# A convolution, scan and attention block on one core: the delta bias as a 49th row of the delta product, and the products of delta and x on GpSimd

## The chip, the cores and the metric

The kernel runs on one core of one Trainium2 chip. The metric is device time in microseconds (us): the median of several executions, without the host. The core has five engines that run side by side and wait for one another through semaphores: TensorE (PE in the profile), VectorE (DVE), ScalarE (ACT), GpSimd (POOL) and SyncE (SP, which issues the transfers here). SBUF is the memory on the chip in which the operands lie. PSUM is the smaller one into which TensorE writes; it has eight banks of 128 x 512 floats.

## The reference, cut to what matters

The block is a state-space layer, then attention, then a mixture of experts. The change lies in the state-space layer. There `x` is convolved and put in four orders (`K = 4`; by rows, by columns, and both backwards). For each order a small matrix gives the step sizes `delta`, through a product of inner size `R = 24`, a bias and a softplus:

```python
x_dbl = jnp.einsum('bkdl,kcd->bkcl', xs, x_proj_w)
dts, Bs, Cs = jnp.split(x_dbl, [R, R + N], axis=2)
dts = jnp.einsum('bkrl,kdr->bkdl', dts, dt_projs_w)
dts = jax.nn.softplus(dts + dt_projs_b[None, :, :, None])
...
dA = jnp.exp(d_t[..., None] * As)
h = h * dA + (d_t * u_t)[..., None] * B_t[:, :, None, :]
```

The scan needs two arrays of it: `delta` and `delta * x`.

## The kernel before

Two images stand side by side on the 128 partitions, so there are two pairs of images (`p` = 0 and 1, `NP = 2`). A pair has 12 **halves** (`HALVES`): one of the four orders and one third of the 192 channels each. A half is 128 partitions by 1024 positions. The 24 halves of both pairs are numbered `m`. They are made in one stretch of the program, called the **delta stage** here; it stands between the input projection with its convolution and the scan.

One half goes through these steps. The lines are those of the profile.

- TensorE multiplies 48 rows of weights (24 for each of the two images) with 48 rows of `rows` into one of two pairs of PSUM banks, `DT_PS[m % 2]` (`delta_product`, L1167). This is two matmuls of 512 columns, and the profile counts four passes, since they are float32.
- ScalarE reads the banks twice, with the bias as an operand: the absolute value goes to `u_mk` (L767), and a biased copy goes to `d_mk` (L768). The copy raises `dt_evacuated`; TensorE waits for it before it fills the same banks for half `m + 2`.
- ScalarE takes exp(-u) (L773). One is added to it, by ScalarE in every third half (`one_more`, L782) and by VectorE in the others (L1618). VectorE keeps what rounding lost (`lost_part`, L1621), ScalarE takes the logarithm (`log_w`, L787).
- VectorE adds max(d, 0) and the logarithm (L1628), subtracts the lost part (L1631), and multiplies with `x` (L1635). SyncE stores both results to HBM (L422, L424), in four buffers (`MADE`).

Softplus is thus max(v, 0) + log(1 + exp(-|v|)).

The order on every engine is written out by hand, in loops over `p` and over a step `s`, and nothing is reordered. Between the halves the same loops carry other work. TensorE makes the rows for the next products and for B and C (`x_proj`, L1139, 12 passes), seven taps of one convolution (`conv`, L1123, 14 passes), and takes away parts that ScalarE has split off (`take_hi`, `take_mid`, L1147). ScalarE splits B and C into three bfloat16 parts (L747, L748, L752, L756), copies `rows` (L737), and once goes through a SiLU block with two table loads (L843 to L846). GpSimd turns `x` by columns (L575). Ahead of the stage VectorE makes the other taps of the convolution (L1572, L1586), and the transfers of the constants, the last of them the four of `xproj_w` (L394), must all have landed before L1650 on VectorE. The tables `HI_AT`, `DT_ROWS_AT`, `BC_ROWS_AT` and `CONV_AT` say after which half each of these stands.

Behind the delta stage follows the scan, 384 units on all engines. VectorE scans (L1705), GpSimd multiplies inputs (L587) and readouts (L604), TensorE spreads B and C (L1213) and adds up (L1229).

Of the kernel before, what the change touches and what calls it, by code (L numbers as in the profile page):

```python
# [5 lines left out]
ALU = mybir.AluOpType  # L6
# [12 lines left out]
H2 = P // 2  # L19
J = DI // H2  # L20
# [3 lines left out]
PART = 3  # L24
DR = 2 * R
SR = 2 * N
BR = PART * SR
# [131 lines left out]
def hybrid_block_kernel(nc, a, out):  # L159
    with ExitStack() as ctx:  # L160
# [21 lines left out]
        a_neg = always.take(OJ, 2, N)  # L182
        dt_bias = always.take(OJ, 2, 1)
        d_sum = always.take(OJ, 1)
# [125 lines left out]
        def attend_bank(i):  # L310
# [13 lines left out]
        ab_ok, u_ok, w_ok, pd_ok = sem("abs_ready"), sem("u_ready"), sem("w_ready"), sem("delta_uncorrected")  # L324
        dtev_ok, lost_ok, ln_ok = (sem(n) for n in ("dt_evacuated", "lost_part", "ln_ready"))
        xd_ok, xa_ok = sem("dt_rows_filled"), sem("bc_rows_filled")
# [36 lines left out]
        CONSTS = [  # L363
            (ident, "ident"), (ones, "ones"), (a_neg, "a_logs"), (dt_bias, "dt_bias"), (d_two, "ds"),
            (conv_b, "conv_b"), (norm_g, "norm_g"), (norm_b, "norm_b"),
# [14 lines left out]
        def _(sp):  # L380
# [181 lines left out]
        def _(pool):  # L562
# [9 lines left out]
            def by_columns(p, j):  # L572
# [109 lines left out]
        def _(act):  # L682
# [74 lines left out]

            def dt_out(p, i):
                k, j, q, dr = half_of(p, i)
                m = p * HALVES + i  # L760
                bias = dt_bias[:, q % OJ, dr, :]
                act.wait_ge(dt_ok, m + 1)
                if m >= MADE:
                    act.wait_ge(dm_st[m % MADE], m // MADE * 32)
                elif m == BLANK_FROM:
# [9 lines left out]
            def one_more(p, i):  # L775
                m = p * HALVES + i
                act.wait_ge(u_ok, m + 1)
                if m:
                    act.wait_ge(pd_ok, m - 1)
                else:  # L780
                    act.wait_ge(xc_ok, J)
                nc.scalar.activation(w_mk[:, m % 2], u_mk[:, m % MADE], ACT.Identity, bias=ones[:, 0:1]).then_inc(w_ok, 1)  # L782
# [280 lines left out]
        def _(pe):  # L1063
# [95 lines left out]
            def delta_product(p, i):  # L1159
                k, j, q, dr = half_of(p, i)  # L1160
                m = p * HALVES + i
                lo = H2 * dr
                pe.wait_ge(rows_ok, p * 2 + k % 2 + 1)
                if m >= 2:
                    pe.wait_ge(dtev_ok, m - 1)
                for h in range(2):
                    mm = pe.matmul(DT_PS[m % 2][:, h * 512:(h + 1) * 512], dt_w[lo:lo + DR, q % OJ, dr],  # L1167
                                   rows[lo:lo + DR, k % 2, h * 512:(h + 1) * 512], start=True, stop=True)
                mm.then_inc(dt_ok, 1)
# [92 lines left out]
            pe.wait_ge(rows_ok, 2 * NP)  # L1262
            pe.wait_ge(dtev_ok, NP * HALVES)
            tile_steps(0, True, False)
# [252 lines left out]
        def _(dve):  # L1517
# [90 lines left out]
            def lost_part(p, i):  # L1608

                m = p * HALVES + i  # L1610
                u, w = u_mk[:, m % MADE], w_mk[:, m % 2]
                if i % J:
                    dve.wait_ge(u_ok, m + 1)
                    if m >= 2:
                        dve.wait_ge(pd_ok, m - 1)
                    else:
                        dve.wait_ge(xc_ok, J)
                    chain.link(nc.vector.tensor_scalar(w, u, 1.0, None, ALU.add))  # L1618
                else:
                    dve.wait_ge(w_ok, m // J + 1)  # L1620
                nc.vector.scalar_tensor_tensor(out=u, in0=w, scalar=-1.0, in1=u, op0=ALU.add, op1=ALU.subtract).then_inc(lost_ok, 1)  # L1621

            def finish(p, i):
                k, j, q, dr = half_of(p, i)
                m = p * HALVES + i
                d, u = d_mk[:, m % MADE], u_mk[:, m % MADE]
                dve.wait_ge(ln_ok, m + 1)
                nc.vector.scalar_tensor_tensor(out=d, in0=d, scalar=0.0, in1=w_mk[:, m % 2],  # L1628
                                               op0=ALU.max, op1=ALU.add).then_inc(pd_ok, 1)
# [21 lines left out]
            for tap in range(PE_TAPS):  # L1651
                nc.vector.tensor_scalar(conv_diag[:, tap], ident, conv_w[:, J - 1, tap:tap + 1], None, ALU.mult)
            nc.vector.tensor_scalar(minus, ident, -1.0, None, ALU.mult)
            nc.vector.tensor_tensor(d_sum.rearrange("p q one -> p (q one)"), d_two[:, 0], d_two[:, 1], ALU.add).then_inc(setup, 1)
            group_var(2)
# [508 lines left out]
```

## Time and profile before

| | |
|---|---|
| time, median of 3 runs | 2245.13 us (2244.14 to 2249.29) |
| span of the profiled execution, first to last instruction | 2244.7 us |
| delta stage in it, from the first L767 to the first product of the scan on VectorE | 95.37 to 253.46 us, 158.1 us |
| VectorE busy in the delta stage | 136.08 us |
| ScalarE busy in the delta stage | 131.63 us |
| TensorE busy in the delta stage | 124.09 us, at a mean granted clock of 0.74 |
| GpSimd busy in the delta stage | 5.68 us |

The profiled execution has no other time than its span; the span lies 0.4 us under the median of the runs. A granted clock of 1.00 is 2.4 GHz for TensorE, and 0.50 is 1.2 GHz. Times in the rows count from the start of the span.

### The profile page before, as it was taken

What the parts mean: (1) busy time and instruction counts of PE and PEld (TensorE: products, weight loads), DVE (VectorE), ACT (ScalarE), POOL (GpSimd) and SP (SyncE); (2) the same over time, 40 slices, a digit from 0 to 9 for tenths busy, and PEclk for the clock granted to TensorE, in tenths of its full rate; (3) what the DMA queues carried; (4) which work ended last, traced back from release to release, by engine and by line L of the source; (5) the groups of instructions that cost most, each with busy time, mean ns of one, the idle gap of its engine ahead of it and who ended that gap; (6) DMA issues with size and microseconds to landing.
All of it is one profiled execution on the core that took longest, in us unless ns stands there. A gap on an engine that the chain in (4) does not pass through costs nothing.

```text
span 2244.7 us, 20167 instructions
## 1 busy us (share of the span) xinstructions
PE 1984.1 (88%) x5826; PEld 919.6 (41%) x5830; DVE 1575.2 (70%) x1505; ACT 1144.9 (51%) x1258; POOL 1297.0 (58%) x464
## 2 busy tenths in 40 slices
PE   7988588888888888888888888989995999999997
PEld 3332133333333333333333333456653555555554
DVE  6978999999999999999999999774553000000000
ACT  4788666666776676776767666211213112122111
POOL 0110499999999999999999999401233011111110
PEclk9987599999999999999999999999997999999999
DMA  6448622233222233222232220611226233333300
GB/s 193 151 175 280 212 75 75 70 98 79 84 66 65 75 100 91 65 75 75 61 105 67 77 73 19 229 42 57 85 85 223 85 119 124 123 119 126 126 24 7
DMA packets 82402, 229.13 MB, mean 102 GB/s; under 512 B 14031, under 2 KB 40257, under 8 KB 80816
## 3 DMA queue, kind: packets, MB, share of 16 engines
q1 hardware_dynamic: 76208, 211.54, 29.6%
q0 software_dynamic: 6144, 16.98, 2.1%
q8 instruction: 24, 0.39, 0.1%
q14 instruction: 26, 0.21, 0.0%
HBM read 166.39 MB, written 64.03 MB: 103 GB/s over the span
## 4 chain that ended last, share of the span: by engine, by line
PE 46%; DVE 23%; issue 17%; POOL 8%; ACT 3%; DMA 1%; DVEq 0%; SPq 0%; ACTq 0%; POOLq 0%
DVE arena L1705 15%; PE ps L1489 11%; PE ps L1502 11%; PE ps L1229 6%; POOL arena L604 4%; POOL arena L587 4%; PE ps L1439 3%; PE ps L1213 2%; PE ps L1110 2%; DVE ps L1688 1%; PE ps L1226 1%; PE ps L1139 1%; PE ps L1390 1%; PE ps L1428 1%; DVE arena L1572 1%
## 5 line engine op out<-in xcount | busy, mean ns | idle before, releaser
L604 POOL TENSOR_TENSOR arena<-arena 128x2048 f32<-128x2048 f32 x192 | 868.3, 4533 | 16.6 <-DVE arena L1705 15.7
L1229 PE MATMUL ps<-arena 128*128 128x512 f32 x1536 | 727.7, 596 | 27.7 <-POOL arena L604 27.6
L1705 DVE TENSOR_TENSOR_SCAN arena<-arena,ps 128x1024 f32<-128x1024 f32 x264 | 587.5, 2266 | 0.0
L880 ACT ACTIVATE arena<-ps 128x1024 f32<-128x1024 f32 x384 | 390.7, 1017 | 248.0 <-PE ps L1213 246.1
L1213 PE MATMUL ps<-arena 96*128 (+1 forms) x1296 | 366.7, 384 | 129.3 <-DVE arena L1705 112.7
L1229 PEld LDWEIGHTS ps<-arena 128*128 128x128 f32 x1536 | 288.4, 190 | 287.7 <-issue 194.0
L587 POOL TENSOR_TENSOR arena<-arena 128x1024 f32<-128x1024 f32 x120 | 283.1, 2359 | 103.5 <-DMA arena<-b_rows 103.5
L2066 DVE TENSOR_TENSOR arena<-ps,arena 128x384 f32<-128x384 f32 x32 | 17.8, 557 | 450.4 <-PE ps L1502 450.4
L1688 DVE TENSOR_TENSOR ps<-ps,arena 128x1024 f32<-128x1024 f32 x264 | 309.1, 1216 | 12.6 <-PE ps L1213 12.6
L873 ACT ACTIVATE arena<-arena 128x1024 f32<-128x1024 f32 x264 | 300.8, 1139 | 8.9 <-DVE arena L1705 8.3
L1213 PEld LDWEIGHTS ps<-arena 96*128 96x128 bf16 x1296 | 112.9, 98 | 461.3 <-DVE arena L1705 215.7
L668 POOL DMA_INDIRECT out<-arena x32 | 31.7, 992 | 437.4 <-DVE arena L2071 437.4
L1705 DVE TENSOR_TENSOR_SCAN arena<-ps,arena 128x1024 f32<-128x1024 f32 x120 | 271.5, 2262 | 4.6 <-ACT ps L873 4.2
L1489 PE MATMUL ps<-arena 128*128 128x512 f32 x576 | 250.2, 595 | 0.0
L1502 PE MATMUL ps<-arena 128*128 128x384 f32 x768 | 250.2, 486 | 0.0
L1502 PEld LDWEIGHTS ps<-arena 128*128 128x128 f32 x768 | 145.4, 190 | 101.5 <-issue 3.8
L873 ACT ACTIVATE ps<-arena 128x1024 f32<-128x1024 f32 x120 | 134.1, 1118 | 88.4 <-DVE arena L1705 88.4
L1489 PEld LDWEIGHTS ps<-arena 128*128 128x128 f32 x576 | 110.1, 191 | 136.8 <-issue 134.4
L1041 ACT ACTIVATE arena<-ps,arena 128x512 f32<-128x512 f32 x96 | 66.0, 688 | 176.0 <-PE ps L1489 175.9
L1048 ACT ACTIVATE arena<-arena 128x384 f32<-128x384 f32 x32 | 16.7, 523 | 232.3 <-DVE arena L2066 232.3
L637 POOL TENSOR_TENSOR arena<-arena 128x384 f32<-128x384 f32 x32 | 27.0, 878 | 185.2 <-DVE arena L1863 185.2
L575 POOL COPY arena<-arena 128x1024 f32<-128x1024 f32 x6 | 13.0, 2192 | 134.2 <-ACT arena L729 134.2
(225 smaller groups left out, 1611.9 us busy)
## 6 DMA issues: line engine op xcount, KB each, us to landing
arena<-b_rows SPq DMA_DIRECT2D x240, 256.0 KB, 4.2
arena<-in_w SPq DMA_DIRECT2D x16, 2304.0 KB, 13.3
delta<-arena SPq DMA_DIRECT2D x24, 512.0 KB, 2.9
delta_x<-arena SPq DMA_DIRECT2D x24, 512.0 KB, 3.1
arena<-delta SPq DMA_DIRECT2D x24, 512.0 KB, 3.6
arena<-delta_x SPq DMA_DIRECT2D x24, 512.0 KB, 4.6
slot_in<-arena SPq DMA_DIRECT2D x8, 772.0 KB, 8.1
arena<-slot_in SPq DMA_DIRECT2D x8, 772.0 KB, 18.0
```

What stands on the lines that cost most here:

```text
L587: nc.gpsimd.tensor_tensor(xin[:, x % XRING], xin[:, x % XRING], dux[:, dr], ALU.mult).then_inc(in_ok, 1)
L604: nc.gpsimd.tensor_tensor(hst[:, h:h + 2], hst[:, h:h + 2], c_sb[:, c:c + 2], ALU.mult).then_inc(p2_ok, 2)
L873: nc.scalar.activation(dst, dlt[:, dr], ACT.Exp, scale=a_neg[:, q % OJ, dr, n:n + 1]).then_inc(dec_ok, 1)
L880: nc.scalar.activation(c_sb[:, u % RING], C_PS, ACT.Copy).then_inc(c_free, 1)
L1041: nc.scalar.activation(h_sb[:, m], ps[:, 3 + m % 3, :], ACT.Gelu_apprx_tanh, bias=b1_col[:, e, m:m + 1]).then_inc(hg_ok, 1)
L1213: mm = pe.matmul(dst[:, h * 512:(h + 1) * 512], sel_lhs[0:BR, n], bc[0:BR, q % OJ // J, dr, m, h * 512:(h + 1) * 512], start=True, stop=True)
L1229: mm = pe.matmul(Y_PS[:, h * 512:(h + 1) * 512], ident, hst[:, u % HRING, h * 512:(h + 1) * 512], start=False, stop=(u == UN - 1))
L1439: mm = pe.matmul(ps[:, attend_bank(i), 0:CA], xnT[:, b % 2, t, i * P:(i + 1) * P], w_eff[:, t], start=(t == 0), stop=(t == CT - 1))
L1489: mm = pe.matmul(ps[:, 3 + m % 3, :], w1[s][:, t, m * P:(m + 1) * P], xeT[:, s, t], start=(t == 0), stop=(t == CT - 1))
L1502: mm = pe.matmul(ps[:, 6 + i % 2, 0:C], h_sb[:, m, i * P:(i + 1) * P], w2[s][:, m], start=(m == 0), stop=(m == MT - 1))
L1688: nc.vector.tensor_tensor(x, x, dux[:, dr], ALU.mult).then_inc(p1_ok, 1)
L1705: nc.vector.tensor_tensor_scan(h, f, x, 0.0, ALU.mult, ALU.add).then_inc(sc_ok, 1)
```

## The change

The biased copy is dropped. Instead the bias becomes a 49th row of the weights (`DRB = 49`), against a 49th row of `rows` that is made to be one, so that the product has the bias in it. The two rows of weights are loaded by two strided transfers of single floats. The sum with max(v, 0) now reads the product in PSUM itself (`whole_delta`), so the banks are free when VectorE has read them (`pd_ok`), no longer when ScalarE has copied them. ScalarE adds the one in every half, and its order in a step is absolute value of half s, logarithm of half s-1, exp and one of half s. The product with `x` leaves VectorE: GpSimd makes it, between its copies by columns.

```diff
+            for lo in (DR, H2 + DR):
+                sp.dma_start(dt_w[lo:lo + 1], a["dt_bias"].rearrange("p q r one -> one q r p"),
+                             allow_slow_non_contiguous=True).then_inc(lb_ok, 16)
...
+            def delta_x(p, i):
+                k, j, q, dr = half_of(p, i)
+                m = p * HALVES + i
+                pool.wait_ge(d_ok, m + 1)
+                u = u_mk[:, m % MADE]
+                nc.gpsimd.tensor_tensor(u, d_mk[:, m % MADE], xy[:, q, :], ALU.mult).then_inc(du_ok, 1)
+
+            for j in range(J):
+                by_columns(0, j)
             for p in range(NP):
-                for j in range(J):
-                    by_columns(p, j)
+                for i in range(HALVES):
+                    delta_x(p, i)
+                    if p == 0 and i == HALVES - 2:
+                        for j in range(J):
+                            by_columns(1, j)
...
-                nc.scalar.activation(rows[0:H2 + DR, o], fill_slot("xd", p, o)[0:H2 + DR], ACT.Copy).then_inc(rows_ok, 1)
+                nc.scalar.activation(rows[0:H2 + DRB, o], fill_slot("xd", p, o)[0:H2 + DRB], ACT.Identity,
+                                     bias=one_row[0:H2 + DRB]).then_inc(rows_ok, 1)
...
-                nc.scalar.activation(u_mk[:, m % MADE], DT_PS[m % 2], ACT.Abs, bias=bias).then_inc(ab_ok, 1)
-                nc.scalar.activation(d_mk[:, m % MADE], DT_PS[m % 2], ACT.Identity, bias=bias).then_inc(dtev_ok, 1)
+                nc.scalar.activation(u_mk[:, m % MADE], DT_PS[m % 2], ACT.Abs).then_inc(ab_ok, 1)
...
                     if s < HALVES:
-                        dt_out(p, s)
-                        exp_abs(p, s)
-                        if s % J == 0:
-                            one_more(p, s)
+                        absolute(p, s)
                     if s >= 1:
                         log_w(p, s - 1)
+                    if s < HALVES:
+                        exp_abs(p, s)
+                        one_more(p, s)
...
                 if m >= 2:
-                    pe.wait_ge(dtev_ok, m - 1)
+                    pe.wait_ge(pd_ok, m - 1)
...
+            def whole_delta(p, i):
+
+                m = p * HALVES + i
+                dve.wait_ge(ln_ok, m + 1)
+                nc.vector.scalar_tensor_tensor(out=d_mk[:, m % MADE], in0=DT_PS[m % 2], scalar=0.0, in1=w_mk[:, m % 2],
+                                               op0=ALU.max, op1=ALU.add).then_inc(pd_ok, 1)
...
                 dve.wait_ge(pd_ok, m + 1)
                 nc.vector.tensor_tensor(d, d, u, ALU.subtract).then_inc(d_ok, 1)
-                if k == 1:
-                    dve.wait_ge(xT_ok, (p + 1) * J)
-                dve.wait_ge(d_ok, m + 1)
-                nc.vector.tensor_tensor(u, d, xy[:, q, :], ALU.mult).then_inc(du_ok, 1)
...
             for p in range(NP):
                 for s in range(HALVES + 1):
+                    if s >= 1:
+                        whole_delta(p, s - 1)
                     if s < HALVES:
                         lost_part(p, s)
```

On ScalarE, late in the second pair, where no other work stands between the halves, a step reads like this before. `delta_stored` is the buffer's store, `dt_filled` the product, `lost_part` VectorE's L1621.

```order
L767 ACTIVATE arena<-ps,arena 128x1024 [waits delta_stored1,dt_filled]
L768 ACTIVATE arena<-ps,arena 128x1024
L773 ACTIVATE arena<-arena 128x1024 [waits abs_ready]
L782 ACTIVATE arena<-arena 128x1024 [waits delta_uncorrected,u_ready]
L787 ACTIVATE arena<-arena 128x1024 [waits lost_part]
```

The same place reads like this after the change. L784 is the absolute value, L801 the logarithm of the half before, L789 the exp and L796 the one.

```order
L784 ACTIVATE arena<-ps 128x1024 [waits delta_stored1,dt_filled]
L801 ACTIVATE arena<-arena 128x1024 [waits lost_part]
L789 ACTIVATE arena<-arena 128x1024 [waits abs_ready]
L796 ACTIVATE arena<-arena 128x1024 [waits delta_uncorrected,u_ready]
L784 ACTIVATE arena<-ps 128x1024 [waits delta_stored2,dt_filled]
```

The copy is gone, and the logarithm of a half has moved behind the absolute value of the next half and ahead of its exp. Before, it stood behind both.

On VectorE, at the same place, one half took these rows before.

```order
L1618 TENSOR_SCALAR arena<-arena 128x1024 [waits delta_uncorrected,u_ready]
L1621 SCALAR_TENSOR_TENSOR arena<-arena 128x1024 [waits dve_chain]
L1628 SCALAR_TENSOR_TENSOR arena<-arena 128x1024 [waits ln_ready]
L1631 TENSOR_TENSOR arena<-arena 128x1024 [waits delta_uncorrected]
L1635 TENSOR_TENSOR arena<-arena 128x1024 [waits delta_ready]
```

After the change VectorE has these rows there: `whole_delta`, the lost part, the subtraction, and `whole_delta` of the next half.

```order
L1635 SCALAR_TENSOR_TENSOR arena<-ps,arena 128x1024 [waits ln_ready]
L1629 SCALAR_TENSOR_TENSOR arena<-arena 128x1024 [waits w_ready]
L1643 TENSOR_TENSOR arena<-arena 128x1024 [waits delta_uncorrected]
L1635 SCALAR_TENSOR_TENSOR arena<-ps,arena 128x1024 [waits ln_ready]
L1629 SCALAR_TENSOR_TENSOR arena<-arena 128x1024 [waits w_ready]
```

Five instructions became three, and the sum with the logarithm now reads PSUM and stands ahead of the next half's lost part.

On TensorE the order is the same; what a product waits for is not. Behind the first rows for B and C, where half 2's product stands with the first `take_hi` behind it, the rows were these before.

```order
L1167 MATMUL ps<-arena 128x512 [waits dt_evacuated,rows_copied]
...
L1147 MATMUL ps<-arena 128x512 [waits b_rows_then_hi]
...
L1167 MATMUL ps<-arena 128x512 [waits dt_evacuated,rows_copied]
...
L1147 MATMUL ps<-arena 128x512 [waits split_mid]
L1147 MATMUL ps<-arena 128x512
L1139 MATMUL ps<-arena 128x512 [waits inproj_out,x_by_columns]
```

They are these after it.

```order
L1183 MATMUL ps<-arena 128x512 [waits delta_uncorrected,rows_copied]
...
L1161 MATMUL ps<-arena 128x512 [waits b_rows_then_hi]
...
L1183 MATMUL ps<-arena 128x512 [waits delta_uncorrected,rows_copied]
...
L1161 MATMUL ps<-arena 128x512 [waits split_mid]
L1161 MATMUL ps<-arena 128x512
L1153 MATMUL ps<-arena 128x512 [waits inproj_out,x_by_columns]
```

The product of half m now waits for `delta_uncorrected` of half m-2, which is `whole_delta`, and `take_hi`, `take_mid` and `x_proj` stay queued behind it.

## Rows read from the trace of the kernel before

**Rows 1.** Stretches: PE, PEld, DVE, ACT, POOL busy (count), PEclk, DMA share, GB/s.

```profile
95.37:253.46 158.09, 124.09 (x223) 44.99 (x226) 136.08 (x122) 131.63 (x133) 5.68 (x3) 0.74 0.59 208
210.00:240.00 30.00, 19.43 (x22) 5.94 (x22) 27.38 (x26) 28.16 (x29) 0.00 (x0) 0.50 0.73 257
```

**Rows 2.** Chain that ended last, 215 to 256 us: start, length, what.

```profile
229.04 1.22 DVE arena L1621
...
245.01 1.22 DVE arena L1621
```

**Rows 3.** Groups by line, 95 to 254 us: count, busy, mean ns, idle ahead.

```profile
L1635 DVE TENSOR_TENSOR arena<-arena 128x1024 f32<-128x1024 f32 x24 | 29.4, 1224 | 1.2
L1621 DVE SCALAR_TENSOR_TENSOR arena<-arena 128x1024 f32<-128x1024 f32 x24 | 29.4, 1224 | 4.2 <-ACT arena L782 3.7
L1628 DVE SCALAR_TENSOR_TENSOR arena<-arena 128x1024 f32<-128x1024 f32 x24 | 29.2, 1218 | 0.0
L767 ACT ACTIVATE arena<-ps,arena 128x1024 f32<-128x1024 f32 x24 | 26.8, 1115 | 10.3 <-PE ps L1167 8.9 <-DMA delta_x<-arena 1.4
L773 ACT ACTIVATE arena<-arena 128x1024 f32<-128x1024 f32 x24 | 25.6, 1066 | 0.0
L787 ACT ACTIVATE arena<-arena 128x1024 f32<-128x1024 f32 x24 | 25.3, 1055 | 7.0 <-DVE arena L1621 7.0
L1618 DVE TENSOR_SCALAR arena<-arena 128x1024 f32<-128x1024 f32 x16 | 11.0, 689 | 15.4 <-ACT arena L773 15.4
L782 ACT ACTIVATE arena<-arena 128x1024 f32<-128x1024 f32 x8 | 9.2, 1148 | 1.2 <-DVE arena L1628 1.0
```

**Rows 4.** TensorE in order of time, 118 to 140 us: start, length, what, passes.

```profile
118.73 1.98 PE L1167 MATMUL ps<-arena 48*128 48x512 f32 x4
...
126.85 1.98 PE L1167 MATMUL ps<-arena 48*128 48x512 f32 x4
```

**Rows 5.** TensorE in order of time, 160 to 235 us.

```profile
167.74 6.76 PE L1139 MATMUL ps<-arena 128*128 128x512 f32 x12
...
201.04 4.23 PE L1167 MATMUL ps<-arena 48*128 48x512 f32 x8
209.02 1.04 PE L1147 MATMUL ps<-arena 128*128 128x512 bf16 x2 [3.75 <-ACT arena L748]
...
225.80 3.75 PE L1167 MATMUL ps<-arena 48*128 48x512 f32 x4 [0.15 <-ACT arena L768]
229.70 3.75 PE L1167 MATMUL ps<-arena 48*128 48x512 f32 x4 [0.15 <-ACT arena L768]
```

**Rows 6.** ScalarE in order of time around the SiLU block, 143 to 156 us.

```profile
144.28 1.28 ACT L843 ACT_TABLE_LOAD   x1
...
150.12 1.11 ACT L767 ACTIVATE arena<-ps,arena 128x1024 f32<-128x1024 f32 x1
```

**Rows 7.** All engines in order of time, 80 to 150 us.

```profile
80.74 12.10 DVE L1586 SCALAR_TENSOR_TENSOR arena<-arena 128x1024 f32<-128x1024 f32 x8
81.29 2.55 POOL L575 COPY arena<-arena 128x1024 f32<-128x1024 f32 x1 [10.41 <-ACT arena L729]
...
93.54 10.53 DVE L1586 SCALAR_TENSOR_TENSOR arena<-arena 128x1024 f32<-128x1024 f32 x8
...
103.99 1.22 DVE L1621 SCALAR_TENSOR_TENSOR arena<-arena 128x1024 f32<-128x1024 f32 x1
```

**Rows 8.** All engines in order of time at the start of the scan, 198 to 262 us.

```profile
256.00 4.64 POOL L587 TENSOR_TENSOR arena<-arena 128x1024 f32<-128x1024 f32 x2 [103.53 <-DMA arena<-b_rows]
```

**Rows 9.** SyncE in order of time, 18 to 30 us.

```profile
21.55 6.46 SPq L394 DMA_DIRECT2D arena<-in_xproj_w  x4
```

**Rows 10.** The stretch behind those transfers (columns as in Rows 1).

```profile
32.00:34.00 2.00, 2.00 (x6) 0.81 (x5) 2.00 (x4) 0.00 (x0) 0.00 (x0) 1.00 0.00 0
```

**Rows 11.** VectorE in order of time, 36 to 46 us.

```profile
37.55 0.25 DVE L1650 TENSOR_SCALAR arena<-arena 128x192 f32<-128x192 f32 x1
...
44.45 2.60 DVE L1572 SCALAR_TENSOR_TENSOR arena<-arena 128x1024 f32<-128x1024 f32 x2 [2.21 <-ACT arena L723]
```

More of the change, by code:

```diff
@@ L25 @@
 DR = 2 * R
+DRB = DR + 1
 SR = 2 * N
@@ L182, in hybrid_block_kernel @@
         a_neg = always.take(OJ, 2, N)
-        dt_bias = always.take(OJ, 2, 1)
+        one_row = always.take(1)
         d_sum = always.take(OJ, 1)
@@ L324, in hybrid_block_kernel @@
         ab_ok, u_ok, w_ok, pd_ok = sem("abs_ready"), sem("u_ready"), sem("w_ready"), sem("delta_uncorrected")
-        dtev_ok, lost_ok, ln_ok = (sem(n) for n in ("dt_evacuated", "lost_part", "ln_ready"))
+        lost_ok, ln_ok, lb_ok = (sem(n) for n in ("lost_part", "ln_ready", "ld_bias_rows"))
         xd_ok, xa_ok = sem("dt_rows_filled"), sem("bc_rows_filled")
@@ L363, in hybrid_block_kernel @@
         CONSTS = [
-            (ident, "ident"), (ones, "ones"), (a_neg, "a_logs"), (dt_bias, "dt_bias"), (d_two, "ds"),
+            (ident, "ident"), (ones, "ones"), (a_neg, "a_logs"), (d_two, "ds"),
             (conv_b, "conv_b"), (norm_g, "norm_g"), (norm_b, "norm_b"),
@@ L756, in split_lo, with absolute @@
                 nc.scalar.activation(parts[:, o, 2], fill_slot("xa", p, o), ACT.Copy).then_inc(lo_ok, 1)
-            def dt_out(p, i):
-                k, j, q, dr = half_of(p, i)
+            def absolute(p, i):
                 m = p * HALVES + i
-                bias = dt_bias[:, q % OJ, dr, :]
                 act.wait_ge(dt_ok, m + 1)
@@ L764, in dt_out @@
                     act.wait_ge(dm_st[m % MADE], m // MADE * 32)
+                elif m == 0:
+                    act.wait_ge(xc_ok, J)
                 elif m == BLANK_FROM:
                     act.wait_ge(zero_st, 16 * E)
-                nc.scalar.activation(u_mk[:, m % MADE], DT_PS[m % 2], ACT.Abs, bias=bias).then_inc(ab_ok, 1)
-                nc.scalar.activation(d_mk[:, m % MADE], DT_PS[m % 2], ACT.Identity, bias=bias).then_inc(dtev_ok, 1)
+                nc.scalar.activation(u_mk[:, m % MADE], DT_PS[m % 2], ACT.Abs).then_inc(ab_ok, 1)
             def exp_abs(p, i):
@@ L777, in one_more @@
                 act.wait_ge(u_ok, m + 1)
-                if m:
+                if m >= 2:
                     act.wait_ge(pd_ok, m - 1)
-                else:
-                    act.wait_ge(xc_ok, J)
                 nc.scalar.activation(w_mk[:, m % 2], u_mk[:, m % MADE], ACT.Identity, bias=ones[:, 0:1]).then_inc(w_ok, 1)
@@ L1164, in delta_product @@
                 if m >= 2:
-                    pe.wait_ge(dtev_ok, m - 1)
+                    pe.wait_ge(pd_ok, m - 1)
+                elif m == 0:
+                    pe.wait_ge(lb_ok, 32)
                 for h in range(2):
-                    mm = pe.matmul(DT_PS[m % 2][:, h * 512:(h + 1) * 512], dt_w[lo:lo + DR, q % OJ, dr],
-                                   rows[lo:lo + DR, k % 2, h * 512:(h + 1) * 512], start=True, stop=True)
+                    mm = pe.matmul(DT_PS[m % 2][:, h * 512:(h + 1) * 512], dt_w[lo:lo + DRB, q % OJ, dr],
+                                   rows[lo:lo + DRB, k % 2, h * 512:(h + 1) * 512], start=True, stop=True)
                 mm.then_inc(dt_ok, 1)
@@ L1262, in _ @@
             pe.wait_ge(rows_ok, 2 * NP)
-            pe.wait_ge(dtev_ok, NP * HALVES)
+            pe.wait_ge(pd_ok, NP * HALVES)
             tile_steps(0, True, False)
@@ L1611, in lost_part @@
                 u, w = u_mk[:, m % MADE], w_mk[:, m % 2]
[L1612 to L1620, printed above, removed]
-                nc.vector.scalar_tensor_tensor(out=u, in0=w, scalar=-1.0, in1=u, op0=ALU.add, op1=ALU.subtract).then_inc(lost_ok, 1)
+                dve.wait_ge(w_ok, m + 1)
+                nc.vector.scalar_tensor_tensor(out=u, in0=w, scalar=-1.0, in1=u, op0=ALU.add, op1=ALU.subtract).then_inc(lost_ok, 1)
+            def whole_delta(p, i):
[3 more added lines that the diff above has]
+                                               op0=ALU.max, op1=ALU.add).then_inc(pd_ok, 1)
             def finish(p, i):
@@ L1626, in finish @@
                 d, u = d_mk[:, m % MADE], u_mk[:, m % MADE]
-                dve.wait_ge(ln_ok, m + 1)
-                nc.vector.scalar_tensor_tensor(out=d, in0=d, scalar=0.0, in1=w_mk[:, m % 2],
-                                               op0=ALU.max, op1=ALU.add).then_inc(pd_ok, 1)
                 dve.wait_ge(pd_ok, m + 1)
                 nc.vector.tensor_tensor(d, d, u, ALU.subtract).then_inc(d_ok, 1)
-                if k == 1:
-                    dve.wait_ge(xT_ok, (p + 1) * J)
-                dve.wait_ge(d_ok, m + 1)
-                nc.vector.tensor_tensor(u, d, xy[:, q, :], ALU.mult).then_inc(du_ok, 1)
             channel_sums(0, xt[:, 0], ld_x[0], 16)
@@ L1653, in _ @@
             nc.vector.tensor_scalar(minus, ident, -1.0, None, ALU.mult)
+            nc.vector.tensor_tensor(one_row, ident[:, DR:DR + 1], ident[:, H2 + DR:H2 + DRB], ALU.add)
             nc.vector.tensor_tensor(d_sum.rearrange("p q one -> p (q one)"), d_two[:, 0], d_two[:, 1], ALU.add).then_inc(setup, 1)
```

## Prediction

> **What bounds the kernel now.** I read the busy times of stretches first. The delta stage takes 158.1 us, and in it VectorE is busy for 136.1, ScalarE for 131.6 and TensorE for 124.1 [rows 1]; no engine is full, so the stage has several limits in turn. Then the chain of waits. Where no other work stands between the halves it runs through VectorE, and three halves lie between the lost parts at 229.04 and 245.01 us, so a half takes 15.97 / 3 = 5.32 us there [rows 2]. That is VectorE's own work: 1.22 for each of L1621, L1628, the subtraction and L1635, and 0.69 for L1618 in two halves of three [rows 3]. TensorE has time to spare: in this stretch its granted clock is 0.50, that is 1.2 GHz, and a product takes 3.75 us [rows 1, 5], but it waits only for ScalarE's copy and so runs ahead of VectorE. In the convolution TensorE is the limit, with 126.85 - 118.73 = 8.12 us a half [rows 4].
>
> **What goes away.** VectorE loses 24 products of 1.224 us and 16 additions of 0.689, together 40.4 us [rows 3]. ScalarE loses 24 biased copies, which have the shape of L767 at 1.115, so 26.8 us, and gets 16 more additions of 1.148, so 18.4 [rows 3]. If the stage ended with VectorE's work, this would be a gain of up to 40 us.
>
> **What the change ties together.** Before, the banks were free when ScalarE had copied them, early in a half. Now they are held until `whole_delta` has read them, and that stands behind the logarithm. And the logarithm of half m stands on ScalarE behind the absolute value of half m+1, which needs the product of m+1, which needs the banks that half m-1 held. So there is a ring, and it turns once in every half: logarithm, `whole_delta`, product two halves on, absolute value, next logarithm. Its length at TensorE's full clock is 1.055 for the logarithm, 1.22 for `whole_delta` (taken as L1628; a read of PSUM that costs more only adds), 1.98 for the product, 1.115 for the absolute value, and 0.15 until TensorE starts after a release: 5.52 us [rows 3 to 5]. At 1.2 GHz the product is 3.75, and the ring 7.29. Both are above the 5.32 of now. What is queued behind the waiting product on TensorE (`take_hi`, `take_mid`, `x_proj`) waits with it, and ScalarE's next split waits for those.
>
> **Which clock.** At 201.04 two products in a row behind an `x_proj` still ran at full clock, 4.23 us for eight passes. At 225.80 and 229.70 products followed each other with 0.15 us between them, and the clock stayed at 1.2 GHz all through the stretch [rows 1, 5]. In the changed kernel products are further apart than that. So I price a half without `x_proj` or convolution ahead of it at 1.2 GHz.
>
> **The 23 steps from one `whole_delta` to the next.**
> - Six halves with nothing between them, the ring alone: 6 x 7.29 = 43.7.
> - Seven halves in which a split stands in the ring: `take_hi` or `take_mid` behind the product, 1.04 [rows 5], and then a copy of ScalarE, some 1.0 as its other instructions of this size [rows 3]: 7 x 9.33 = 65.3. (Four splits touch two halves each; one of these eight falls on an `x_proj`.)
> - Two halves beside the convolution: 8.12 as now [rows 4], since the convolution covers the ring: 16.2.
> - Five halves with an `x_proj` between two products. It begins at the low clock and takes 6.76 [rows 5], with a product of 1.98 and 0.15 behind it 8.9, or 10.7 if the product is slow too; I take 9.3, nearer to the first, for TensorE has just worked without a gap: 46.5.
> - The half with the SiLU block, 150.12 - 144.28 = 5.84 [rows 6], beside a logarithm, exp, addition, absolute value and two copies: 5.84 + 1.06 + 1.07 + 1.15 + 1.12 + 2.0 = 12.2.
> - The last half of each pair, where no absolute value stands ahead of the logarithm: 1.06 + 1.07 + 1.15 + 1.22 = 4.5, twice 9.0.
>
> Together 192.9. The first lost part starts at 103.99 as now, behind the taps [rows 7], so the first `whole_delta` ends at 103.99 + 1.22 + 1.06 + 1.22 = 107.5 and the last at 300.4. The last subtraction (1.22) and a wait for GpSimd's port (0 to 1.2, I take 0.6) put the scan's first product at 302.2, against 253.46 now: 48.7 us later.
>
> **What lies beside other work.** GpSimd makes its 24 products at 2.32 us (4.64 for two of the same shape), and idles for 103.5 us until the scan now [rows 8]; even with its three copies by columns in between it needs less than half of a step of 7.29. SyncE's store of a product comes 1 to 2 us later than now, and the loads of the scan's first rows stand behind the store of half 22; this costs 0 to 1 us at the start of the scan, nothing in the sum. GpSimd and VectorE get in each other's way: eight taps took 12.10 us while GpSimd copied for 2.55, and 10.53 while it did not [rows 7]. In a half the two would share 2.32 + 1.22 + 1.22 = 4.8 us one after the other, which is under the ring at either clock. Bounds for it: nothing, and 24 lost parts each held up for a whole product, 24 x 2.32 = 56 us. At 1.2 GHz the lost part is ready 1.06 + 1.07 + 1.15 + 1.22 = 4.5 after the logarithm before it and is wanted at 7.29, so it can be held up for 2.8 without loss; I take nothing.
> The Trainium skill, SBUF — State Buffer, Who interferes with whom, speaks against the move: the two engines share a pair of ports, and a VectorE instruction with two SBUF inputs (the lost part, the subtraction) and a GpSimd instruction that reads SBUF exclude each other for the whole instruction. The taps agree, with 1.57 us lost to one copy. By this rule taken at its worst the sum would have the 56 us in it, by the slack of 2.8 it has none.
> The two rows of bias are 3072 runs of one float, and they stand ahead of the four transfers of `xproj_w`, which have as many runs of 256 bytes. Those are issued from 21.55, and no transfer runs after 32.0 [rows 9, 10], so they take 10.5 at most. The constants are wanted at 37.55, and VectorE idles for another 2.21 later [rows 11]: cover of 7.8 us. Bounds: 0, if single floats are quick, and 2 x 10.5 - 7.8 = 13 late, if each costs twice such a run; as long as the other four they would be 2.7 late. I take 0, since they move a 64th of the bytes.
>
> **The sum.** The span of the profiled execution is 2244.7; with 48.7 it is 2293.4. The median of the runs lies 0.4 above that span, so 2294.
>
> **The rivals.**
> - *TensorE keeps its full clock in the ring.* Then the halves are 6 x 5.52, 7 x 7.0 (half a `take`, one copy), 16.2, 5 x 7.4 (`x_proj` at 5.3, from 8.12 - 1.98 for 14 passes), 12.2 and 9.0, together 156.5: 36.4 less, and 2258. For it: the clock came back in every convolution. Against it: the two products without a gap at 1.2 GHz [rows 5]. Chance 0.07.
> - *The clock stays low in `x_proj` and the convolution too*, at 3.75 / 4 a pass: some 15 a half for five, 17 for two, 15 for the SiLU half, together 243, so 2344; or the bias comes late, up to 2307. Chance 0.10 for both; only the upper end of it leaves the range.
> - *GpSimd holds up the lost parts.* If other waits push each product just ahead of a lost part, and the ring has no slack left, up to 56 us come on top, and 2350. For it: rows 7. Against it: a slack of 2.8 a half, which a product of 2.32 does not fill. Chance 0.04. This is the port rule of the Trainium skill's SBUF page at its worst.
> - *VectorE's relief decides, and the kernel is faster.* The stage would lose up to 40.4 us, which gives 2205. It decides from the point where the ring is shorter than 5.32, that is where a product takes under 1.78 us; the shortest in the rows is 1.98. It could be so if ScalarE got ahead in a way that I do not see. Chance 0.06, of which 0.02 for a gain that only evens out.
> - *The forecast*, with the clock at 1.2 GHz in most halves: 0.73. Its own range is 2278 to 2310, by two steps' worth of clock either way.
>
> **Numbers.** 2294, range 2262 to 2322. Left out are the first rival (0.07), the far end of the second (0.03), GpSimd at its worst (0.04) and VectorE's relief (0.06). A change within 0.2% (4.5 us) is about what a measurement of this kernel cannot tell from none. Faster 0.04, same 0.02, slower 0.94.
>
> **What the profile after would show.** The delta stage grows from 158 to about 207 us; TensorE's product has VectorE's `whole_delta` as its releaser in nearly all of the 22 waits, and ScalarE's absolute value has the product. Late in the second pair the lost parts lie 7.3 apart, with VectorE busy for half of that. The granted clock there is 0.50. GpSimd's products lie beside it, and the scan takes as long as now. I am wrong if the lost parts lie 5.3 apart or closer, if the product is released by something other than `whole_delta`, if the clock there is 1.00, or if time appears ahead of 95 us, behind the constants.

## The result, and the profile after

The changed kernel takes 2291.62 us (median of 4 runs, 2290.17 to 2292.31), the kernel before 2245.08. The ratio is 1.0203, with a 95% interval of 1.0189 to 1.0218: 46.5 us slower, where 2294 was predicted. The span of the profiled execution is 2288.4 us. It lies 3.2 us under the median: each execution's time is 1.8 above its own span (this one took 2290.17), and this one was the fastest of the four. A second execution profiled later has a span of 2290.1.

The first group shows two stretches of the kernel after, with the columns of [rows 1]: the whole delta stage, and the late second pair.

```profile
94.77:296.20 201.43, 130.96 (x222) 46.78 (x222) 100.42 (x82) 123.16 (x123) 61.60 (x26) 0.70 0.44 159
255.00:290.00 35.00, 16.68 (x19) 4.79 (x18) 15.65 (x14) 20.86 (x21) 11.71 (x5) 0.50 0.48 178
```

The stage has grown from 158.1 to 201.4 us, although VectorE has 35.7 us less to do in it (136.1 to 100.4) and ScalarE 8.5 less. In the late stretch no engine is busy for more than 60% of the time: 20.86 of 35 on ScalarE, 16.68 on TensorE, 15.65 on VectorE. When no engine is full, each waits for another in turn. The chain of waits of the kernel after says what (start, length, what):

```profile
268.17 3.76 PE ps L1183 x4
271.93 0.02 issue
271.96 1.02 ACT arena L784
272.98 0.95 ACT arena L801
273.93 0.02 issue
273.96 1.24 DVE arena L1635
275.19 0.14 issue
275.33 3.76 PE ps L1183 x4
```

This is the ring: product, absolute value, logarithm of the half before, `whole_delta`, and the product two halves on. It closes after 275.33 - 268.17 = 7.16 us. Before, the chain stayed on VectorE here, at 5.32 a half [rows 2]. The waits of the kernel after, 95 to 297 us, name the same links (total us, times, longest):

```profile
POOL arena L587 <- DVE arena L1643: 151.5, 23, 27.1
...
DVE arena L1635 <- ACT arena L801: 78.3, 22, 8.6
PE ps L1183 <- DVE arena L1635: 62.5, 13, 9.3
ACT arena L784 <- PE ps L1183: 30.4, 11, 4.0
```

And these are its groups by line, 94 to 300 us, which answer to [rows 3]:

```profile
L1183 PE MATMUL ps<-arena 49*128 49x512 f32 x91 | 67.3, 879 | 62.5 <-DVE arena L1635 62.5
L587 POOL TENSOR_TENSOR arena<-arena 128x1024 f32<-128x1024 f32 x24 | 56.3, 2346 | 151.5 <-DVE arena L1643 151.5
...
L1629 DVE SCALAR_TENSOR_TENSOR arena<-arena 128x1024 f32<-128x1024 f32 x24 | 30.7, 1280 | 22.4 <-ACT arena L796 22.4
L1635 DVE SCALAR_TENSOR_TENSOR arena<-ps,arena 128x1024 f32<-128x1024 f32 x24 | 29.4, 1225 | 78.3 <-ACT arena L801 78.3
L796 ACT ACTIVATE arena<-arena 128x1024 f32<-128x1024 f32 x24 | 27.6, 1148 | 0.8
L801 ACT ACTIVATE arena<-arena 128x1024 f32<-128x1024 f32 x24 | 25.3, 1053 | 4.1 <-DVE arena L1629 4.1
...
L784 ACT ACTIVATE arena<-ps 128x1024 f32<-128x1024 f32 x24 | 24.5, 1022 | 30.4 <-PE ps L1183 30.4
```

No instruction has become much longer. `whole_delta` takes 1.225 us from PSUM, as L1628 did from SBUF. What is new are the idle times at the end of the rows: 62.5 us of TensorE and 78.3 of VectorE.

From the starts of the 24 `whole_delta`s the 23 steps can be read and set against the prediction (us):

| steps | predicted, each and together | measured | together |
|---|---|---|---|
| 6 plain | 7.29, 43.7 | five of 7.16, one of 6.68 | 42.5 |
| 7 with a split | 9.33, 65.3 | 9.04 | 63.3 |
| 2 beside the convolution | 8.12, 16.2 | 8.12 | 16.2 |
| 5 with an `x_proj` | 9.3, 46.5 | 6.80, 6.99, 9.66, 9.71, 9.81 | 43.0 |
| SiLU block | 12.2 | 13.1 | 13.1 |
| 2 last of a pair | 4.5, 9.0 | 4.48 | 9.0 |
| sum | 192.9 | | 187.0 |

In the kernel before, the same 23 steps, from L1628 to L1628, took 140.5 us.

### The profile page after: what moved, and what is told of

Its sections match the earlier page's. It is cut to its first block, busy times and chain, and to the rows that moved or that the text cites. A ratio compares the mean times of both kernels' runs of the same rounds, so it can differ in the third digit from the quotient of the medians.

```text
span 2288.4 us, 20143 instructions
## 1 busy us (share of the span) xinstructions
PE 1993.7 (87%) x5830; PEld 920.5 (40%) x5830; DVE 1539.5 (67%) x1466; ACT 1140.7 (50%) x1250; POOL 1354.9 (59%) x488
## 4 chain that ended last, share of the span: by engine, by line
PE 48%; DVE 22%; issue 16%; POOL 8%; ACT 4%; DMA 1%; DVEq 0%; ACTq 0%; POOLq 0%; SPq 0%
DVE arena L1715 14%; PE ps L1505 11%; PE ps L1518 11%; PE ps L1245 6%; POOL arena L620 4%; POOL arena L603 4%; PE ps L1455 3%; PE ps L1183 3%; PE ps L1229 2%; PE ps L1153 2%; DVE arena L1588 1%; DVE ps L1698 1%; PE ps L1242 1%; PE ps L1406 1%; PE ps L1444 1%
## 5 line engine op out<-in xcount | busy, mean ns | idle before, releaser
L1698 DVE TENSOR_TENSOR ps<-ps,arena 128x1024 f32<-128x1024 f32 x264 | 309.2, 1217 | 12.2 <-PE ps L1229 12.2
L603 POOL TENSOR_TENSOR arena<-arena 128x1024 f32<-128x1024 f32 x120 | 283.1, 2360 | 3.4 <-DMA arena<-b_rows 3.4
L587 POOL TENSOR_TENSOR arena<-arena 128x1024 f32<-128x1024 f32 x24 | 56.3, 2346 | 151.5 <-DVE arena L1643 151.5
```

The lines of the kernel that those rows point to most:

```text
L603: nc.gpsimd.tensor_tensor(xin[:, x % XRING], xin[:, x % XRING], dux[:, dr], ALU.mult).then_inc(in_ok, 1)
L1698: nc.vector.tensor_tensor(x, x, dux[:, dr], ALU.mult).then_inc(p1_ok, 1)
```

## The experiments

The theory: the held banks close a ring whose product runs at 1.2 GHz, and this is the whole loss. Its rivals: GpSimd's use of the SBUF ports that it shares with VectorE; the new order and the additional ones on ScalarE; the transfers of the bias rows. Ratios are to the kernel before, and all experiments change either the kernel before or the kernel after, as each says.

**wait_only: the wait alone.** The kernel before, with one line changed.

```diff
-                    pe.wait_ge(dtev_ok, m - 1)
+                    pe.wait_ge(pd_ok, m - 1)
```

> The kernel before with one wait changed: the product waits for the sum with the logarithm of two halves earlier, not for ScalarE's biased copy. Theory (holding the banks closes a ring): the ring here is sum 1.22 + start of TensorE 0.15 + product 3.75 + absolute value 1.115 + copy 1.115 + exp 1.066 + add and lost part 1.91 = 10.3 us a half instead of 5.32, over most of the 23 steps; I expect 2342 us (2310 to 2365), later than the changed kernel, since its order on ScalarE is the worse one for the ring. Rival (the engines' busy time decides, the wait is covered): 2245 to 2255 us.

2344.47 us, ratio 1.0443 (1.0426 to 1.0460). The waits of wait_only, 95 to 346 us, begin, apart from the queues', with:

```profile
PE ps L1167 <- DVE arena L1628: 104.5, 19, 10.7
...
ACT arena L767 <- PE ps L1167: 54.6, 11, 6.2
```

So one wait, with not an instruction more or less, costs 99.6 us. A plain step has 10.1 us. The ring is shown. In the changed kernel it costs less, 46.5: there the copy is gone from it, and by the new orders on ScalarE and VectorE the exp, the added one and the lost part stand outside it. How much of the difference each of these makes was not tested.

**pool_only and pool_32_columns: GpSimd's part alone.** The kernel before with VectorE's product taken out and `delta_x` on GpSimd, as in the change; the second one with the product cut to 32 columns and all waits left.

```diff
-                nc.vector.tensor_tensor(u, d, xy[:, q, :], ALU.mult).then_inc(du_ok, 1)
...
+                nc.gpsimd.tensor_tensor(u, d_mk[:, m % MADE], xy[:, q, :], ALU.mult).then_inc(du_ok, 1)
...
+                nc.gpsimd.tensor_tensor(u[:, 0:32], d_mk[:, m % MADE, 0:32], xy[:, q, 0:32], ALU.mult).then_inc(du_ok, 1)
```

> The kernel before with only the products of delta and x moved to GpSimd. Theory: VectorE's 5.32 us a half falls to 4.1, and ScalarE's 2 x 1.115 + 1.066 + 1.148/3 + 1.055 = 4.73 bounds the plain halves; some 0.5 us in 13 steps and a later start of the scan behind the last product give 2237 us (2228 to 2244). Rival (GpSimd's use of the shared port holds VectorE up): 2245 to 2260 us. Rival (VectorE's relief counts in full): 2216 us.

> The kernel before with the product of delta and x moved to GpSimd, which multiplies only the first 32 of the 1024 columns, so delta times x is wrong in the others; all waits are as in the whole move, which took 2260.8 us. Theory (GpSimd's product shuts VectorE's lost part out while it runs): without it the lost part falls from 2.20 us to 1.22, and the time to 2235 us (2226 to 2243), VectorE's relief without its price. Rival (the extra link from VectorE over GpSimd to the store makes the loss): 2252 us or more.

pool_only takes 2260.79 us, ratio 1.0066 (1.0049 to 1.0083): I had expected a gain of 8, and it lost 16. pool_32_columns takes 2238.73, ratio 0.9964 (0.9950 to 0.9978). So the relief of VectorE is worth 7 us, and GpSimd's product while it runs costs 22. In both kernels an `x_proj` also waits for GpSimd's copies by columns, which now stand behind products in its order, for 5.8 us in pool_only and 3.0 in pool_32_columns; the 7 us are what is left beside that. The time line of pool_only, of VectorE and GpSimd late in the stage (start, length; the first and fourth row are the add and the sum), shows how:

```profile
252.32 0.69 DVE L1630 TENSOR_SCALAR arena<-arena 128x1024 f32<-128x1024 f32 x1
252.48 2.73 POOL L583 TENSOR_TENSOR arena<-arena 128x1024 f32<-128x1024 f32 x1 [2.42 <-DVE arena L1643]
253.04 3.25 DVE L1633 SCALAR_TENSOR_TENSOR arena<-arena 128x1024 f32<-128x1024 f32 x1
256.21 1.21 DVE L1640 SCALAR_TENSOR_TENSOR arena<-arena 128x1024 f32<-128x1024 f32 x1
257.46 1.22 DVE L1643 TENSOR_TENSOR arena<-arena 128x1024 f32<-128x1024 f32 x1
258.76 2.72 POOL L583 TENSOR_TENSOR arena<-arena 128x1024 f32<-128x1024 f32 x1 [3.55 <-DVE arena L1643]
```

The lost part starts at 253.04 and ends at 256.29, 1.08 after GpSimd has ended at 255.21: nearly its whole 1.22 us lie behind that end, as if it had stood still until then. VectorE's 4.35 us of work a half (0.69 + 3 x 1.22) have become a step of 258.76 - 252.48 = 6.28, more than the 5.32 before. Over the stage the mean lost part takes 2.19 us in pool_only and 1.26 in pool_32_columns. This is what the Trainium skill states in SBUF — State Buffer, Who interferes with whom: a VectorE instruction with two SBUF inputs and a GpSimd instruction that reads SBUF contend, and the one that begins later is blocked until the other has ended. The trace agrees: GpSimd began first here, and in the same trace, at 246.71, a product that began 0.07 us behind a lost part took 3.36 us.

**vector_product: the product back on VectorE.** The kernel after, without `delta_x` on GpSimd and with VectorE's line as before.

> The changed kernel with the products of delta and x back on VectorE. Theory (the ring through the banks is the whole loss, GpSimd's part costs and gives nothing): VectorE's idle time in a plain step, 2.67 us, takes the 1.22 of the product; 2290 us (2286 to 2294). Rival (GpSimd's port makes part of the loss): down to 2250 us. Rival (VectorE's time still counts): 2305 to 2320 us.

2292.45 us, ratio 1.0208 (1.0191 to 1.0225), the same as the changed kernel. The time line of VectorE in it (L1623 is `whole_delta`, L1635 the product):

```profile
273.67 1.22 DVE L1617 SCALAR_TENSOR_TENSOR arena<-arena 128x1024 f32<-128x1024 f32 x1 [0.90 <-ACT arena L784]
274.81 1.22 DVE L1631 TENSOR_TENSOR arena<-arena 128x1024 f32<-128x1024 f32 x1
276.13 1.23 DVE L1635 TENSOR_TENSOR arena<-arena 128x1024 f32<-128x1024 f32 x1
278.70 1.23 DVE L1623 SCALAR_TENSOR_TENSOR arena<-ps,arena 128x1024 f32<-128x1024 f32 x1 [1.34 <-ACT arena L789]
```

With the product in it VectorE still waits 1.34 us for the logarithm; in the changed kernel it waits 2.67. The ring made room for a product on either engine, and so GpSimd's product neither gave nor cost anything there.

**copy_back: the banks released early again.** The kernel after, with a copy of ScalarE behind the absolute value, which releases the banks; the sum reads the copy.

```diff
+                nc.scalar.activation(d_mk[:, m % MADE], DT_PS[m % 2], ACT.Copy).then_inc(dtev_ok, 1)
...
-                    pe.wait_ge(pd_ok, m - 1)
+                    pe.wait_ge(dtev_ok, m - 1)
...
-                nc.vector.scalar_tensor_tensor(out=d_mk[:, m % MADE], in0=DT_PS[m % 2], scalar=0.0, in1=w_mk[:, m % 2],
+                nc.vector.scalar_tensor_tensor(out=d_mk[:, m % MADE], in0=d_mk[:, m % MADE], scalar=0.0, in1=w_mk[:, m % 2],
```

> The changed kernel with the copy out of the banks back on ScalarE, without a bias since the 49th row has it, and the banks released by it; the sum reads the copy. Theory: the ring is open, ScalarE's 1.02 + 1.02 + 1.05 + 1.05 + 1.15 = 5.3 us bounds a plain half, and the time is that of before, 2243 us (2235 to 2250). Rival (the new order on ScalarE or the ones that moved there make the loss): 2280 us or more.

2257.80 us, ratio 1.0055 (1.0037 to 1.0072). With one instruction more in every half 34 us are back, and the products wait for the copy (19.3 us in the stage), no longer for the sum. I had expected all 46. The 23 steps are still 10.5 us longer than in the kernel before, and two things lie there. One is GpSimd's price as in pool_only: over the stage the mean sum takes 1.83 us and the mean lost part 1.58, for 1.22 without GpSimd. The other is an `x_proj` of the second pair that waits for GpSimd's copies by columns (L579), which the change put behind eleven of its products; the step behind it takes 10.72 us, for 7.02 before. The groups of copy_back, 94 to 275 us, have this wait:

```profile
L1154 PE MATMUL ps<-arena 128*128 128x512 f32 x84 | 43.5, 674 | 5.3 <-POOL arena L579 5.3
```

How much each of them costs was not taken apart. In its time line (VectorE and GpSimd) the sum, which now has two inputs in SBUF, stands still beside GpSimd:

```profile
237.62 2.35 POOL L587 TENSOR_TENSOR arena<-arena 128x1024 f32<-128x1024 f32 x1 [3.46 <-DVE arena L1644]
237.95 3.10 DVE L1636 SCALAR_TENSOR_TENSOR arena<-arena 128x1024 f32<-128x1024 f32 x1 [0.41 <-ACT arena L802]
```

In the kernel after, `whole_delta` has one input in PSUM, and beside the same product of GpSimd neither of the two takes longer (1.22 and 2.36); the subtraction behind it, with two inputs in SBUF, does (time line of the kernel after):

```profile
292.75 1.22 DVE L1635 SCALAR_TENSOR_TENSOR arena<-ps,arena 128x1024 f32<-128x1024 f32 x1
292.84 2.36 POOL L587 TENSOR_TENSOR arena<-arena 128x1024 f32<-128x1024 f32 x1 [4.81 <-DVE arena L1643]
294.00 2.27 DVE L1643 TENSOR_TENSOR arena<-arena 128x1024 f32<-128x1024 f32 x1
```

**half_product and product_twice: the product as a link, and its clock.** The kernel after, with half and with twice the passes.

```diff
-                for h in range(2):
+                for h in range(2 if m < 2 else 1):
...
+                for h in (0, 1, 0, 1):
```

> The changed kernel in which the product of every half behind the first two makes only the first 512 of its 1024 columns, so delta is wrong in the others. Theory (the product at 1.2 GHz is a link of the ring): 1.87 us less in each of 13 plain and split steps, and in some three steps behind an x_proj where it ran at the low clock too; a plain step goes from 7.16 to 5.3 us and the time from 2291.6 to 2264 us (2257 to 2270). Rival (the releaser is named by the trace but something else sets the step): 2285 us or more. Rival (the slack of the ring was also what hid GpSimd's products): the step falls by less than 1.87, 2272 to 2284 us, with lost parts of over 1.5 us.

> The changed kernel with every product made twice into the same banks, so with eight passes. Theory (TensorE is at 1.2 GHz in the ring and every microsecond of the product counts in full): 3.75 us more in 13 plain and split steps, some 2 in the two beside the convolution and some 3 in the five with an x_proj, 65 to 70 us in all, 2360 us (2345 to 2368). Rival (with twice the work the clock goes to 2.4 GHz, so eight passes take 8 / 4 x 1.98 = 3.96 us, what four took): 2292 to 2305 us.

half_product takes 2266.65 us, ratio 1.0087 (1.0071 to 1.0104), 25 us less than the changed kernel. product_twice takes 2354.19, ratio 1.0479 (1.0460 to 1.0498), 62.6 more. TensorE in order of time, late in half_product:

```profile
252.62 2.04 PE L1183 MATMUL ps<-arena 49*128 49x512 f32 x2 [3.41 <-DVE arena L1635]
258.07 2.04 PE L1183 MATMUL ps<-arena 49*128 49x512 f32 x2 [3.41 <-DVE arena L1635]
```

The step is 5.45 where it was 7.16: the 1.71 us that the product lost (3.75 to 2.04), all of them. And in product_twice, with a stretch of it in the columns of [rows 1]:

```profile
320.97 7.16 PE L1183 MATMUL ps<-arena 49*128 49x512 f32 x8 [3.41 <-DVE arena L1635]
331.53 7.16 PE L1183 MATMUL ps<-arena 49*128 49x512 f32 x8 [3.41 <-DVE arena L1635]
```

```profile
310.00:345.00 35.00, 24.39 (x28) 8.85 (x29) 13.14 (x12) 13.29 (x13) 7.02 (x3) 0.50 0.31 112
```

The step is 10.56, longer by just what the product grew (7.16 - 3.75 = 3.41). The idle time ahead of a product is 3.41 in both, and in the changed kernel it was 7.16 - 3.75, the same: it is the rest of the ring, and doesn't depend on the product. The granted clock of the stretch is still 0.50, so twice the passes didn't bring the clock back.

**log_first: the order on ScalarE.** The kernel after, with the logarithm ahead of the next absolute value again.

```diff
-                    if s < HALVES:
-                        absolute(p, s)
                     if s >= 1:
                         log_w(p, s - 1)
                     if s < HALVES:
+                        absolute(p, s)
                         exp_abs(p, s)
```

> The changed kernel with the logarithm of a half put back ahead of the absolute value of the next one on ScalarE; the banks are still held until the sum with the logarithm. Theory (the ring closes in one step only because the logarithm stands behind the next absolute value): the ring now spans two steps of 10.8 / 2 = 5.4, and ScalarE's logarithm, absolute value, exp and one with VectorE's lost part behind them bound a plain step at 5.7; some 27 us less over the 23 steps, 2265 us (2255 to 2275). Rival (holding the banks costs the same in any order): 2285 us or more.

2277.15 us, ratio 1.0139 (1.0123 to 1.0155), 14.5 less than the changed kernel: about half of what I expected, and outside of both ranges. The plain steps are 5.53, near the 5.7 of the theory and 1.63 less than in the changed kernel; but the seven steps with a split still take 8.13, only 0.91 less. There ScalarE stands with a split that waits for TensorE's `take`, and that is queued behind the product (246.95 to 250.70), ahead of which TensorE had idled 3.41 us for the banks (time line of log_first, TensorE and ScalarE):

```profile
250.63 1.03 PE L1160 MATMUL ps<-arena 128*128 128x512 bf16 x2
...
251.70 1.02 ACT L773 ACTIVATE arena<-ps 128x1024 bf16<-128x1024 f32 x1 [2.98 <-PE ps L1160]
```

So the order loosens the ring, but doesn't open it: the splits close it again by another way.

**after_again and bias_behind: the bias rows' transfers.** The kernel after once more, and with the two transfers moved behind the four of `xproj_w`.

> The changed kernel once more, beside the kernel whose only difference is the place of the bias rows' transfers. In the profiles so far the constants land at 40.6 to 45.4 us in kernels with the bias rows, and by 38.4 or earlier in those without. If that differs from one execution to the next, this profile shows another landing than 40.6, and the median is again 2291.6 us (2289 to 2294).

> The changed kernel with the two transfers of the bias rows behind the four of the x_proj weights, where no constant waits for them. Theory (the single floats hold up the last constants by more than the cover behind them): the constants land by 38.5 us as in the kernel before, the first lost part starts at 103 to 104, and the time is 2289 us (2287 to 2290.5), 1 to 4 us less than the changed kernel in the same rounds. Rival (the cover hides them, as the prediction took it): the same median within 1 us.

2291.86 us (2290.24 to 2295.46) and 2291.77 (2290.01 to 2292.02), ratios 1.0205 (1.0191 to 1.0219) and 1.0198 (1.0185 to 1.0212): no difference, against my theory of 1 to 4 us. The transfers do delay the constants. VectorE's first instruction behind them, in the kernel after, in after_again, and in bias_behind:

```profile
40.63 0.26 DVE L1657 TENSOR_SCALAR arena<-arena 128x192 f32<-128x192 f32 x1 [3.56 <-DMA arena<-in_xproj_w]
```

```profile
42.23 0.26 DVE L1657 TENSOR_SCALAR arena<-arena 128x192 f32<-128x192 f32 x1 [3.21 <-DMA arena<-in_xproj_w]
```

```profile
37.20 0.25 DVE L1657 TENSOR_SCALAR arena<-arena 128x192 f32<-128x192 f32 x1
```

But the first `whole_delta` starts at 105.71, 109.03 and 106.00, and the last at 292.75, 296.25 and 296.33. In bias_behind an `x_proj` at 120.91 takes 7.68 us, in the other two 6.01 and 6.11, and two later ones are slower by 0.8 and 0.2. So in bias_behind the early start was given back within the stage. Whether it always is was not measured; the medians say that on the whole it costs nothing.

**row_balanced and row_by_step: what of the change can be kept.** The bias as a 49th row, with the copy (now without bias) still releasing the banks, the order on ScalarE and VectorE as before, and the product on VectorE. In row_balanced ScalarE adds the one in three halves of four. In row_by_step VectorE adds it in the 14 halves where ScalarE also has a split or rows to copy, and the bias rows stand behind `xproj_w`.

```diff
-                        if s % J == 0:
+                        if (p, s) not in VEC_ONES:
                             one_more(p, s)
```

> The kernel before with the half of the change that needs no bank held: the bias as a 49th row, so that the absolute value (1.02 for 1.115 us) and the copy (1.02 for 1.115) need none, ScalarE adds the one in three halves of four instead of one of three, and everything else as before. Theory: VectorE's plain step goes from 5.32 to 4 x 1.22 + 0.69 / 4 = 5.06 us, ScalarE's to 5.02; 0.26 us in some 13 steps, 2241.5 us (2238 to 2245). Rival (ScalarE becomes the bound with its splits, or the bias rows come late): 2246 us or more.

> The bias as a 49th row without its two prices: ScalarE's copy still frees the banks, VectorE still makes the products of delta and x, and the bias rows' transfers stand behind those of the x_proj weights. VectorE adds the one in the 14 halves in which ScalarE also has a split or rows to copy, ScalarE in the other ten. Theory (the bias rows cost what row_balanced lost, and each engine is relieved where it is the bound): 2241 us (2237.5 to 2244.5). Rival (in most steps neither VectorE nor ScalarE is the bound alone): 2244.5 to 2247 us, no difference from before.

row_balanced takes 2246.10 us, ratio 1.0004 (0.9995 to 1.0014), no gain where I had expected 3 to 4 us; row_by_step 2242.61, ratio 0.9988 (0.9979 to 0.9997), 2.1 us under the kernel before. That is the fastest complete version, by about what can be told from none. In row_balanced the bias is a 49th row and the loss is gone, so the row itself is not its cause. What copy_back still loses against it, some 12 us, goes with GpSimd's work and the new orders together.

## Why the prediction was right

Point by point, by its own steps:

- **The ring.** Right in its links, its order and its length: 7.16 us for 7.29. The 0.13 are the absolute value, which without a bias takes 1.02 (predicted with the shape of L767, 1.115), and the logarithm, which starts 0.1 before the absolute value's end in the records. The product counts in full, as half_product and product_twice show; the links that wait_only adds count in full together (10.1 for 10.3). The others were not changed one by one.
- **The clock.** Right: 0.50 in the late stretch, and products of 3.75. The rival with the full clock is out; even twice the passes don't raise it.
- **The steps.** Splits 9.04 for 9.33. The largest error is the `x_proj` steps, 43.0 for 46.5. The product behind ran at the full clock in all five (1.98), where a price between the two clocks was taken. In the two steps of 6.8 and 7.0 the `x_proj` had begun 3.2 us before the step did, so less of it counted; the other three began later or held copies of ScalarE too. The SiLU step was 0.9 longer. The sum came out 5.9 too high. TensorE in the steps from 123.79 and from 231.90:

```profile
120.63 6.01 PE L1153 MATMUL ps<-arena 128*128 128x512 f32 x12
126.57 1.98 PE L1183 MATMUL ps<-arena 49*128 49x512 f32 x4
...
229.79 7.82 PE L1153 MATMUL ps<-arena 128*128 128x512 f32 x12
237.54 1.98 PE L1183 MATMUL ps<-arena 49*128 49x512 f32 x4
```

- **The ends.** The first `whole_delta` ended at 106.9 for 107.5. From the end of the last one to the scan's first product it took 2.2 for 1.8, since GpSimd held the last subtraction up for 1.05 (2.27 in the row at 294.00). The scan's first product stands at 296.20, 42.7 later than before for the 48.7 predicted.
- **SyncE's loads at the scan's start**, taken as 0 of 0 to 1: they cost 1.5 us there, more than the upper bound. The chain of waits of the kernel after runs through them, and the third scan then waits for GpSimd (second fence, VectorE's time line):

```profile
296.17 5.76 DMA arena<-b_rows
...
302.08 2.35 POOL arena L603
```

```profile
304.45 2.29 DVE L1715 TENSOR_TENSOR_SCAN arena<-ps,arena 128x1024 f32<-128x1024 f32 x1 [1.53 <-POOL arena L603]
```

  The span is 43.7 us longer, 1.0 more than the scan's start, where the sum said 48.7. That 2294 came within 2.4 us is in part luck: the span was taken 5.0 too long, and the median lies 3.2 above the profiled span, for the 0.4 assumed.
- **The bias rows**, taken as 0 of 0 to 13: the constants let VectorE go on at 40.6 to 45.4 us in the eight kernels with them ahead, and it did not wait there, at 37.2 to 38.9, in the six in which they are not ahead; but the medians of the two kernels that differ in nothing else are equal. Right in the time; the reason given, that they move few bytes, was wrong. Time ahead of the stage, named as a sign of being wrong, does not show in the kernel after (first lost part at 103.37, for 103.99 before), but 1.3 us of it show in after_again (105.31).
- **GpSimd**, taken as nothing because a slack of 2.8 a half covers it: right in the time, as vector_product shows. But in a plain step the lost part is not held up at all: the product begins at 271.36, right behind the subtraction, and its 2.34 us lie within the 2.67 in which VectorE waits for the logarithm. The rival's mechanism is real, though. Where the ring doesn't give the slack it costs 22 us (pool_only against pool_32_columns).
- **What would be seen.** "In nearly all of the 22 waits" was wrong in the count: TensorE idles for `whole_delta` 13 times. The other products follow an `x_proj`, the convolution or another product without a gap.

## What to carry to other kernels

A buffer is not only memory: whoever reads it last sets when its writer may go on. Before a copy out of PSUM is saved, follow what then stands between the product and its last reader, and back to the next product; if that ring is longer than the busiest engine's work for a turn, the copy was cheap. Work moved to an idle engine has to be priced with what it shuts out while it runs, and a measurement inside a kernel that waits for something else will not show that price.

## What was not expected of the hardware

- A VectorE sum with one input in PSUM runs beside a GpSimd product undisturbed (1.22 us, and 2.36 for the product), and the same sum with both inputs in SBUF takes 3.10. The Trainium skill states this in SBUF — State Buffer, Who interferes with whom: with at most one SBUF input, and outside its two-port modes, a VectorE instruction doesn't contend with GpSimd. The trace agrees.
- Two transfers of 12 KB together, in 3072 single floats, held up VectorE's first use of the constants behind them by 3.6 us in the kernel after and by 8.5 in half_product (idle time ahead of L1657); in bias_behind, where they stand behind, it did not wait.
- TensorE stayed at 1.2 GHz (granted clock 0.50) with pieces of work of 7.16 us and 3.41 us between them, in product_twice.
